# Attention with grouped heads: the last four output projections of a kv group moved from its end to between the first scores of the next group

## What is computed

```python
q = einsum('bim,ghmd->bghid', ln(x), w_aq)   # G, H = 4, 4 (kv groups, heads per group), D = 128
k = einsum('bim,gmd->bgid', ln(x), w_ak); v = einsum('bim,gmd->bgid', ln(x), w_av)
q, k = rope(q) * D**-0.25, rope(k) * D**-0.25
p = softmax(q @ k.T + causal mask)           # per b, g, h: 1024 x 1024, lower triangle
r = einsum('bghid,ghdm->bim', p @ v, w_ao)   # summed over all groups and heads
x2 = x + ln(r)
```

## Time and profile before

| | us |
|---|---|
| median of three runs (lowest, highest) | 3695.26 (3694.72, 3696.39) |
| the profiled execution, its own time | 3691.28 |
| its span, first to last instruction | 3689.5 |
| attention groups, first projection to the last group's start | 38.27 to 2330.96 |
| a common group | 151.5 to 152.3 |
| PE busy over the span | 3404.8 (92%) |
| DVE, POOL, ACT busy | 2179.4, 1715.9, 1630.7 |

### The profile page before, as it was taken

One profiled execution on the slowest core, in us unless ns is written; L12 is line 12 of the kernel. 1 busy time (PEld: TensorE's weight loads), 2 busy tenths in 40 slices (PEclk: granted clock), 3 DMA queues, 4 the chain that ended last, 5 costly groups with the idle time before them and its releaser, 6 DMA issues. The chain is left out here.

```text
span 3689.5 us, 73909 instructions
## 1 busy us (share of the span) xinstructions
PE 3404.8 (92%) x20374; PEld 2907.5 (79%) x20375; DVE 2179.4 (59%) x4740; ACT 1630.7 (44%) x3672; POOL 1715.9 (47%) x2208
## 2 busy tenths in 40 slices
PE   6999999999999999999999999985898999999987
PEld 5888888888888888888788888874687777777766
DVE  6665665656656566565665656656664454544448
ACT  2543545435344353543545435343122554554544
POOL 2534435444354343544435444355422555555548
PEclk9999999999999999999999999995899999999999
DMA  2111103201021210210312101026332887888877
GB/s 85 61 36 39 53 24 104 70 30 55 22 64 41 99 55 21 64 41 31 101 45 65 41 31 55 28 78 227 103 112 78 186 196 175 187 183 179 184 161 276
DMA packets 232277, 339.92 MB, mean 92 GB/s; under 512 B 20800, under 2 KB 106048, under 8 KB 231136
## 3 DMA queue, kind: packets, MB, share of 16 engines
q1 hardware_dynamic: 198624, 244.43, 20.3%
q0 software_dynamic: 33280, 91.02, 12.4%
HBM read 225.00 MB, written 110.38 MB: 91 GB/s over the span
## 5 line engine op out<-in xcount | busy, mean ns | idle before, releaser
L588 DVE TENSOR_TENSOR ptl<-TP,pth 128x512 fp32r<-128x512 f32 (+1 forms) x640 | 407.4, 636 | 253.4 <-ACT pth L746 243.6
L746 ACT CAST pth<-TP 128x512 fp32r<-128x512 f32 (+1 forms) x640 | 347.2, 549 | 310.4 <-PE TP L923 307.5
L838 PE MATMUL O<-pth,vh 128*128 128x256 f32 (+1 forms) x1280 | 402.6, 314 | 26.8 <-DVE ptl L588 23.6
L576 DVE TENSOR_REDUCE negmax<-S 128x1 f32<-128x384 f32 (+7 forms) x512 | 378.9, 747 | 20.6 <-PE S L908 14.6
L838 PE MATMUL S<-kTh,qTh 128*128 128x512 f32 (+3 forms) x768 | 305.8, 398 | 70.2 <-ACT prob L738 32.6
L404 POOL TENSOR_TENSOR work<-work,cst 128x320 f32<-128x320 f32 x128 | 132.9, 1038 | 502.0 <-ACT work L730 502.0
L840 PE MATMUL O<-pth,vl 128*128 128x256 f32 (+1 forms) x1280 | 359.4, 281 | 0.0
L839 PE MATMUL O<-ptl,vh 128*128 128x256 f32 (+1 forms) x1280 | 359.1, 281 | 0.0
L838 PE MATMUL S<-wph,xTh 128*128 128x512 f32 (+1 forms) x1024 | 353.9, 346 | 3.5 <-DVE xTl L529 1.7
L839 PE MATMUL S<-wpl,xTh 128*128 128x512 f32 (+1 forms) x1024 | 346.4, 338 | 0.0
L840 PE MATMUL S<-wph,xTl 128*128 128x512 f32 (+1 forms) x1024 | 345.2, 337 | 0.0
(11 more groups left out here) (320 smaller groups left out, 9514.1 us busy)
## 6 DMA issues: line engine op xcount, KB each, us to landing
raww<-in_L_ffn_w_dram SPq DMA_DIRECT2D x95, 512.0 KB, 9.0
stage<-in_L_attn_w_aq_dram SPq DMA_DIRECT2D x68, 256.0 KB, 3.0
stage<-in_L_attn_w_ao_dram SPq DMA_DIRECT2D x64, 256.0 KB, 2.6
work<-in_L_attn_x_dram SPq DMA_DIRECT2D x64, 256.0 KB, 2.7
xt_d<-work SPq DMA_DIRECT2D x64, 256.0 KB, 2.8
a<-acc_d SPq DMA_DIRECT2D x64, 256.0 KB, 4.1
h_d<-work SPq DMA_DIRECT2D x40, 256.0 KB, 3.1
acc_d<-x SPq DMA_DIRECT2D x1, 8448.0 KB, 31.8
```

The lines of the kernel that those rows point to most:

```text
L576: nc.vector.tensor_reduce(negmax[:, n % 4:n % 4 + 1], S[:, a, 0:(IB * ib + a + 1) * P], AX_X, ALU.max, negate=True).then_inc(max_ready, 1)
L588: nc.vector.tensor_tensor(ptl[:, n % 2, 0:w], TP[:, n % 2, 0:w], pth[:, n % 2, 0:w].bitcast(F32), ALU.subtract).then_inc(tp_lo, 1)
L746: nc.scalar.copy(pth[:, n % 2, 0:w], TP[:, n % 2, 0:w]).then_inc(tp_hi, 1)
L838: mm(out, ah, bh, start=first, stop=False)
```

## The change

PE's loop over the four groups is written out, and DVE's as well, so that each of the four can differ. The last four projections of groups 0 to 2 of a batch are taken out of the group's end, and each is issued in the next group's head: behind scores(0, 0), scores(0, 1), scores(1, 0) and scores(1, 1). In the last group of a batch they stay behind its last unit. `OUTPUTS` starts with them, and the counts of `o_free` and `r_done` are shifted by four. DVE's additions follow: behind row_max(0, 0) with the end of the rotation of tile 7 and `lo_tile(6)`, behind row_max(1, 0), row_max(1, 1) and lo_pair(0). The additions of group 0's late tiles, now in group 1, are the copies.

Beside this: ACT's copy to slotB goes to POOL, ahead of its subtraction and with a wait between the two; POOL splits the next weights at units 7, 8, 9, 11 (two) and 13, where it did at 7, 9, 11 (two), 13 and 15; it waits for the loaded xT at unit 13 and no longer after 15; SP stores `racc` within the next batch's first group, behind the load of the second x tile. Loops on ACT and POOL are unchanged.

```diff
-OUTPUTS = [x for u in range(len(UNITS)) for x in [("r", t) for t in PROJECT_AT.get(u, [])] + [("o", u)]]
-OUTPUTS += [("r", t) for t in PROJECT_LAST]
+OUTPUTS = [("r", t) for t in PROJECT_LAST]
+OUTPUTS += [x for u in range(len(UNITS)) for x in [("r", t) for t in PROJECT_AT.get(u, [])] + [("o", u)]]
...
                 sp.dma_start(slotD, x_t[nt[1]]).then_inc(xa_in, 16)
+                if first:
+                    wait_apart(sp, o_free, b * (G * MG) + (len(PROJECT_LAST) + 2))
+                    sp.dma_start(r_d[held((b + B - 1) % B)].rearrange("(t p) m -> p t m", p=P), racc[:]).then_inc(r_out, 16)
                 load_out(it, g, (2,))
...
                         if u in X_LOW:
                             wait_apart(pool, xp_hi, it * SIDE + (X_LOW[u] + 2))
+                            nc.gpsimd.tensor_scalar(slotB.bitcast(F32R), slotC, 1.0, 1.0, ALU.mult, ALU.mult).then_inc(pl, 1)
+                            wait_apart(pool, pl, pl0 + (5, 8)[X_LOW[u]])
                             nc.gpsimd.tensor_tensor(slotC.bitcast(F32R), slotC, slotB, ALU.subtract).then_inc(xp_lo, 1)
...
-                            n = IB * (u % 2 + 1) if u >= HALFU else 0
+                            n = len(PROJECT_LAST) + (IB * (u % 2 + 1) if u >= HALFU else 0)
                             pool.wait_ge(r_done, it * NT + n + 1)
...
-                        for n in {7: (0,), 9: (1,), 11: (2, 3), 13: (4,), 15: (5,)}.get(u, ()):
+                        for n in {7: (0,), 8: (1,), 9: (2,), 11: (3, 4), 13: (5,)}.get(u, ()):
                             split_proj(n, it * 10 + 10, it * 80 + 80)
...
                     rope_end(NT - 1)
                     lo_tile(NT - 2)
+                    if g:
+                        add_results(PROJECT_LAST[0:1], copies == "last")
                     row_max(0, 1)
                     row_max(1, 0)
+                    if g:
+                        add_results(PROJECT_LAST[1:2], copies == "last")
                     lo_tile(NT - 1)
                     row_max(1, 1)
+                    if g:
+                        add_results(PROJECT_LAST[2:3], copies == "last")
                     recips(0)
                     lo_pair(0)
+                    if g:
+                        add_results(PROJECT_LAST[3:4], copies == "last")
...
-                iteration(b, 0, True)
-                with v.Fori(1, G) as g:
-                    iteration(b, g, False)
+                for g in range(G):
+                    iteration(b, g, {0: "middle", 1: "last"}.get(g, ""))
...
-                            nc.scalar.copy(slotB.bitcast(F32R), side)
                             nc.scalar.copy(slotC, side).then_inc(xp_hi, 1)
...
-                with pe.Fori(0, G) as g:
+                for g in range(G):
...
                     transpose_tile(NT - 3)
                     scores(0, 0)
+                    if g:
+                        out_project(PROJECT_LAST[0])
                     transpose_tile(NT - 2)
                     scores(0, 1)
+                    if g:
+                        out_project(PROJECT_LAST[1])
                     scores(1, 0)
+                    if g:
+                        out_project(PROJECT_LAST[2])
                     transpose_tile(NT - 1)
                     scores(1, 1)
+                    if g:
+                        out_project(PROJECT_LAST[3])
                     transpose_pair(0)
...
-                    for t in PROJECT_LAST:
-                        out_project(t)
+                    if g == G - 1:
+                        behind, mb = pe.snap(it + 1), pe.snap(m0 + MG)
+                        for t in PROJECT_LAST:
+                            project_out(t, behind, mb)
```

More of the change, by code:

```diff
@@ L97 @@
 PROJECT_LAST = [IB * ib + a for ib in BLOCKS[1] for a in range(IB)]
-OUTPUTS = [x for u in range(len(UNITS)) for x in [("r", t) for t in PROJECT_AT.get(u, [])] + [("o", u)]]
-OUTPUTS += [("r", t) for t in PROJECT_LAST]
+OUTPUTS = [("r", t) for t in PROJECT_LAST]
+OUTPUTS += [x for u in range(len(UNITS)) for x in [("r", t) for t in PROJECT_AT.get(u, [])] + [("o", u)]]
 PROJECTED = [n for kind, n in OUTPUTS if kind == "r"]
-FINAL = PROJECTED
+FINAL = PROJECTED[len(PROJECT_LAST):] + PROJECT_LAST
 SCALED = [(k, i - k) for i in range(NT + 1) for k in range(2) if 0 <= i - k < NT]
@@ L224, in attention @@
         N = B * G
-        Z4, Z2, ZP, ZT, ZX, ZD, ZO = 4 * N, 2 * N, 20 * N + 1, NT + N * TG, SIDE * N, 10 * N, 16 + 32 * N
+        Z4, Z2, ZP, ZT, ZX, ZD, ZO = 4 * N, 2 * N, 22 * N + 1, NT + N * TG, SIDE * N, 10 * N, 16 + 32 * N
         block = ctx.enter_context(nc.Block())
@@ L255, in _, with iteration @@
             load_proj(0, 0, range(2, MC + 2))
-            sp.wait_ge(rwT_sb, 3)
-            sp.dma_start(r_d[B - 1].rearrange("(t p) m -> p t m", p=P), racc[:]).then_inc(r_out, 16)
             def held(e):
                 return e if isinstance(e, int) else sp.snap(e)
-            def iteration(b, g):
+            def iteration(b, g, first):
                 it = held(b * G + g)
@@ L313, in iteration @@
                 store_h(1)
[L315 to L321, removed]
+            with sp.Fori(0, B) as b:
+                iteration(b, 0, True)
+                with sp.Fori(1, G) as g:
+                    iteration(b, g, False)
             sp.wait_ge(tp_done, NT + B * G * TG)
@@ L406, in iteration @@
                     for u, (ib, h) in enumerate(UNITS):
-                        pl0 = it * 20 + 1
+                        pl0 = it * 22 + 1
                         if u == RELOAD and reload:
@@ L421, in iteration @@
                             wait_apart(pool, str_ready, it * 4 + k * 2 + 2)
-                            norm_scale(pl0, pl, 6 + 8 * k, mva[:, k, 0:1], mva[:, k, 1:2], sch[:, k], mr[:, k], scr_ready)
+                            norm_scale(pl0, pl, 8 + 8 * k, mva[:, k, 0:1], mva[:, k, 1:2], sch[:, k], mr[:, k], scr_ready)
                         if u in R_STAT:
@@ L449, in iteration @@
                             pool.wait_ge(s_done, it * SG + NT)
-                        for n in {7: (0,), 9: (1,), 11: (2, 3), 13: (4,), 15: (5,)}.get(u, ()):
+                        for n in {7: (0,), 8: (1,), 9: (2,), 11: (3, 4), 13: (5,)}.get(u, ()):
                             split_proj(n, it * 10 + 10, it * 80 + 80)
[L453 to L457, removed]
+                        if reload and u == 13:
+                            landed = pool.to_reg(b * 32 + 32)
+                            pool.wait_ge(xt_in, 32)
+                            pool.wait_ge(xt_in, landed)
+                            pool.sem_inc(xt_ready, 1)
             with pool.Fori(0, B - 1) as b:
@@ L478, in _ @@
             v.sem_inc(tp_lo, 2)
-            v.sem_inc(o_free, 2)
+            v.sem_inc(o_free, 2 + len(PROJECT_LAST))
             for name in (xt_out, x2_out, h_out):
@@ L595, in norm_out, with add_results @@
                                                 ALU.mult).then_inc(o_free, 1)
-                    def add_results(tiles):
+                    def add_results(tiles, copies=False, it=it):
                         for t in tiles:
@@ L649, in iteration @@
                             if jp == 0 and ib == 0:
-                                add_results(PROJECT_AT.get(u, []))
+                                add_results(PROJECT_AT.get(u, []), copies == "middle")
                             if n < NPAIR:
@@ L662, in iteration @@
                         norm_out(u)
-                    add_results(PROJECT_LAST)
+                    if g == G - 1:
+                        add_results(PROJECT_LAST, it=v.snap(it + 1))
             with v.Fori(0, B) as b:
-                iteration(b, 0, True)
-                with v.Fori(1, G) as g:
-                    iteration(b, g, False)
+                for g in range(G):
+                    iteration(b, g, {0: "middle", 1: "last"}.get(g, ""))
             sums = [0]
@@ L676, in linked @@
                 v.wait_ge(dl, ZD + sums[0])
-            v.wait_ge(o_free, B * G * MG + 2)
+            v.wait_ge(o_free, N * MG + (len(PROJECT_LAST) + 2))
             for i in range(NT + 4):
@@ L840, in mm3, with project_out @@
                 return mm(out, al, bh, start=False, stop=last)
+            def project_out(t, it, m0):
+                ib, a = t // IB, t % IB
+                late = t in PROJECT_LAST
+                pe.wait_ge(o_free, m0 + (OUTPUTS.index(("r", t)) + 1))
+                if a == 0:
+                    last = -1 if late else max(u for u in range(len(UNITS)) if UNITS[u][0] == ib)
+                    pe.wait_ge(o_split, it * len(UNITS) + (last + 1 + 1))
+                    pe.wait_ge(stage_free, it * 10 + (2 if late else 12))
+                for h in range(H):
+                    place = ib // (NIB // 2), h, slice(a * P, (a + 1) * P)
+                    ins = mm3(bank("r", t), oTh[:, *place], oTl[:, *place], woh[:, h], wol[:, h], h == 0, h == H - 1)
+                ins.then_inc(r_done, 1)
             pe.sem_inc(pv_done, 2)
```

(3 more changed lines are left out.)

2 lines of the change are left out of this document (1 added, 1 removed).

## The result

The kernel after takes 3629.13 us (four runs, 3626.67 to 3632.85) against 3695.56 for the kernel before beside it (3694.72 to 3696.39). The ratio is 0.9828, with a 95% interval of 0.9816 to 0.9840: 66 us faster where 58 were forecast. The profiled run's span is 3624.9 us. Over all its runs the kernel before moved between 3682.59 and 3701.14 us, its medians on four occasions between 3690.54 and 3695.56, so a few us of what follows can't be told apart by the medians. The traces tell more. Attention is taken here from the start of the first projection to the start of the last matmul of the last late projection: 2444.00 us in the trace of before (38.27 to 2482.27), 2379.60 after (36.62 to 2416.22), so 64.4 us less.

A forecast was written before the change was run, and what follows sets the result against it. PE's own order of work was taken to bound the kernel, leaving its idle and low-clock time to win. 39.5 + 3.5 + 15.0 = 58.0 us gives 3637 us for the median, range 3620 to 3660.

The forecast's parts named there:

- Part 1: Heads of the 12 groups not first in a batch: four moved projections fill PE's gaps, 3.29 us each, 39.5 us.
- The three gaps: PE's idle time in a head: 1.04 us before tile 6's transposes, 1.41 before scores(1, 0), 0.84 before scores(1, 1).
- the 0.56: PE's idle 0.56 us in a head before the first product with v; expected to stay as it is.
- Part 2: Group at 1414.02 and the next: with head gaps filled, no clock fall; 3.5 us won, bounds 0 and 4.2.
- Part 3: Units 2 and 4: without ACT's first side-tile copy, the signal to PE's scores comes 0.47 us earlier, 32 times, 15.0 us.
- Part 4: A group's end: what its 11.20 us of projections covered (weights, ACT's loop, racc store, xT wait); no loss counted.
- (a): POOL's last weight split, moved from unit 15 to 13, ends 3.36 us before it is wanted, so project(0) needn't wait.
- (b): ACT's loop end and table load at a group's end: its first copy is 0.24 us late, taken as 0.
- rival D: Slower: project(0) of the 12 groups waits 5.2 us for the sixth weight split; 3699 us, chance 0.03.
- The loops: Loops over groups written out: 0 us won, at most 1.5, as PE's inner ends show no gap.
- rival E: PE's back edges were a cost that shows as no gap: 29 us more won, 3608 us, chance 0.01.
- Rival C: Last group of a batch: POOL's wait for a load behind xT's 4 MB goes too; 6.5 us, 3630.5, chance 0.13.

The follow-up runs named there:

- e4_tail: e1_wait14 with the four late projections back behind the last unit in all 16 groups: 3655.38 us, ratio 0.9905 to the kernel before.
- e1_wait14: The kernel after, with tile 0's projection behind a batch's last unit waiting for POOL's split of unit 14, not 15: 3613.23 us, ratio 0.9791.
- e3_pool_copy: The kernel before with only the side tile's first copy moved from ACT to POOL: 3677.85 us, ratio 0.9954.
- e2_act_copy: The kernel after with the side tile's first copy back on ACT and POOL's copy gone: 3644.90 us, ratio 0.9879.
- e7_unrolled: The kernel before with only PE's and DVE's loops over the groups written out: 3678.81 us, ratio 0.9958.
- e5_old_splits: e1_wait14 with POOL's weight splits at the units of before (7, 9, 11, 11, 13, 15): 3698.03 us, ratio 1.0013.
- e8_reload9: e1_wait14 with POOL's 4 MB load of the next batch's xT issued at unit 9, one unit later: 3608.57 us, ratio 0.9773.
- e9_all: The kernel after with the unit 14 wait, the fourth late projection behind the first transposes of probabilities, and xT's load at unit 9: 3604.55 us, ratio 0.9761.

## Why the prediction was right, and where not

| term of the sum | forecast | by the medians | attention in the traces |
|---|---|---|---|
| head of 12 groups, with the clock | 43.0 | 42.2 (e4_tail less e1_wait14) | 47.2 |
| one copy less on ACT | 15.0 | 13.9 (e3_pool_copy), 15.8 (e2_act_copy) | 15.2, 16.8 |
| loops written out | 0, at most 1.5 | 12.9 (e7_unrolled) | 11.6 |
| wait at a batch's end | none | 14 to 16 lost (e1_wait14, by the ratios) | 13.6 lost |
| sum | 58.0 | 53 to 55 | 60.4 |
| the kernel | 58 | 66.4 and 60.1 | 64.4 |

The sum of the measured terms takes 13.9 and 15.2 for the copy. It falls short of the kernel by 4 us in the traces and by more in the medians, whose errors of several us a term add up. Groups at the full clock add up better: 3.80 for the head, 1.02 for two copies (e2_act_copy against the kernel after) and 0.64 for the loops are 5.46 us a common group, where it lost 5.35 in the pair above and 5.40 on average.

**Part 1, the head,** held. The three gaps went, the 0.56 stayed, and DVE's additions and the changes of work cost 0.1 us a head at most. The idle rows were a lower bound: 3.29 where the matmuls' starts show 3.90 and the groups 3.80, since a bracket leaves out the stretch from a start to its modelled end.

**Part 2, the clock.** In the profiled run after, the 12 heads show 1.00, as expected. In the kernel before, one more of these heads, in the group at 191.40, had a stretch at 0.50 (from 233.2 to 236.6), which the prediction did not list; that group took 151.86 us, 0.2 over the common one. The price of 3.5 was not measured apart; e5_old_splits shows how large it can be, some 2.7 us per group, when a gap of 4.4 stands in each.

**Part 3, the copy,** held within 2 us: a wait of 0.79 became 0.3, as worked out, and no new wait of PE for POOL came with it.

**Part 4, what loses its cover.** (a) and (b) came out as worked out. The split ended 3.37 ahead (forecast 3.36), and ACT's table load was just ahead of its first copy. The rival D, the late weights, was a real danger: with the splits in their old places the kernel is slower than before. Its price was too low, since the clock falls behind each wait. The step that failed is "In the last group of a batch the late projections stand where they stood". They stood there with another wait, and it cost some 14 us. I read the moved calls and not the condition in the new function that they share: `last` is -1 for every late tile, which is right in the head and too strong behind the last unit.

**The loops** were the term that was mis-sized. I took "no gap is reported" for "no cost". The bound from the rows was 1.5 us, and the runs give 12.9. The reading was wrong as well: two of the 12 inner ends have a bracket of 0.20 and 0.23 us, at 1414.02 and 1721.53, and six more are late without one. The Trainium skill, Runtime: NRT & Kernel Launch, "Instruction fetch mechanics", says that a taken branch to a page that is not held costs a fetch. The direction agrees with these runs, the size that I drew for it from ACT's idle time (29, rival E) does not, and no run here shows that a fetch is the cause. DVE's part turned up as an earlier exponential in the middle of a group, not at the branch.

The two misses, some +12 and -14, nearly cancel, so it is luck that the total came out so close. **Rival C**, the late landing, stayed in the kernel after (its group at 1064.71 is 163.96 us long, 3.7 over the last group at 471.48), and e8_reload9 and e9_all took it away by issuing the 4 MB behind the small load.

## What to carry to other kernels

Work that nobody waits for was worth most here in the places where PE runs dry in a ring of short steps: there it cost at most 0.1 us a head, and the clock no longer fell in these heads. Read such a place from start to start of matmuls, since the idle time in brackets is too small. Before moving work, list what it covered where it stood: here the moved weight splits carried twice what the moved projections won. And when one function comes to serve two places, check its waits for each place, since the stronger one is paid in both.

## What the runs showed that was not expected

- A hardware loop whose back edge mostly shows no gap still cost time: 7.9 us for 12 inner edges on PE, 2.8 of them at the edges from start to start, and 3.7 for 8 on DVE, which waits for ACT there anyway (4.63 us, till 500.24).
- A gap of 4.37 us on PE costs more than itself: granted clock 0.50 in the 4 us around the restart and 0.71 in the next, some 2.7 us on top, and so in each of 12 groups in a row. The gaps of 1.04 and 1.41 us in the heads of the kernel before brought it down in 4 of 16 groups only, and the gap of 2.45 at a batch's end in one of four batches of this trace of the kernel after.
- A small load of 256 KB on SP's queue, issued at 1200.40 just behind 4 MB on POOL's (1199.40 and 1200.04), landed 15.6 us later, where the median of such loads is 2.7, and held POOL for 12.11 us; with the 4 MB issued one unit later, these waits are 3.0 us in all.
